# Six of a layer's 391 gathered tiles fetched row by row from the sync queue

## The reference

```python
xw = x @ W                                            # 3125 x (2*128)
xj = xw[src].reshape(-1, H, D) + edge_emb.reshape(-1, H, D)
xi = xw[dst].reshape(-1, H, D)
alpha = leaky_relu(einsum('ehd,hd->eh', xi, att_i) + einsum('ehd,hd->eh', xj, att_j))
ea = exp(alpha - segment_max(alpha, dst)[dst])
alpha = ea / (segment_sum(ea, dst)[dst] + EPS)
aggr = segment_sum(xj * alpha[..., None], dst)        # random rows by src, sums by dst
h = aggr.mean(axis=1) + b                             # relu between layers; self loops are added
```

## Time and profile before

| | |
|---|---|
| median of the runs | 3281.18 us |
| profiled execution | 3286.07 us, of which the span is 3284.3 us |
| TensorE matmul busy | 2403.9 us (73%), mean granted clock 0.543 |
| VectorE busy | 2048.8 us (62%) |
| ScalarE busy | 669.4 us (20%) |
| GpSimd busy | 2140.9 us (65%), of it 1871.6 us in 1955 gathers |
| DMA | 195.81 MB, mean 60 GB/s |

### The profile page before, as it was taken

How to read it: one execution, slowest core, us unless ns; L and a number is a source line. 1 busy time by engine, 2 the same in 40 slices (tenths; PEclk the granted TensorE clock), 3 DMA queues, 4 the chain that set the end, 5 groups by cost and what they waited for, 6 DMA issues and landing times.

```text
span 3284.3 us, 48911 instructions
## 1 busy us (share of the span) xinstructions
PE 2403.9 (73%) x13595; PEld 1980.3 (60%) x13595; DVE 2048.8 (62%) x6821; ACT 669.4 (20%) x3102; POOL 2140.9 (65%) x2357
## 2 busy tenths in 40 slices
PE   6879954778776678768578777857777685778768
PEld 6769933656665456657356656636656573556657
DVE  8965465566576566566656565665565575566567
ACT  0048831111114111110411111131111122111112
POOL 0047737777765777774677777477777747777772
PEclk9555555555557555555755555575555566555556
DMA  3211112222221222221122222122222212222221
GB/s 102 102 69 58 58 51 58 61 60 62 63 51 42 59 64 59 60 64 44 48 64 59 59 66 58 36 59 61 59 62 65 56 36 58 61 62 59 59 56 52
DMA packets 114125, 195.81 MB, mean 60 GB/s; under 512 B 39897, under 2 KB 77272, under 8 KB 113864
## 3 DMA queue, kind: packets, MB, share of 16 engines
q0 software_dynamic: 62560, 130.25, 18.0%
q1 hardware_dynamic: 51304, 62.42, 5.8%
HBM read 180.86 MB, written 11.67 MB: 59 GB/s over the span
## 4 chain that ended last, share of the span: by engine, by line
POOL 50%; issue 18%; DVE 15%; PE 14%; DMA 2%; ACT 1%; DVEq 1%; POOLq 0%; ACTq 0%
POOL ring L512 49%; PE bank L751 6%; PE bank L753 3%; PE bank L724 2%; DVE prod L1079 2%; DVE ring L854 2%; DMA ring<-table,srci 2%; POOL ring L493 1%; DVE ai_rows L947 1%; PE bank L747 1%; DVE y L1361 1%; DVE y L1367 1%; DVE acc L951 1%; DVE prod L1331 1%; PE bank L652 1%
## 5 line engine op out<-in xcount | busy, mean ns | idle before, releaser
L512 POOL DMA_INDIRECT ring<-table,srci x1955 | 1871.6, 957 | 633.6 <-issue 583.0
L751 PE MATMUL bank<-pw,ring 128*128 128x48 f32 x3910 | 1216.9, 411 | 0.0
L751 PEld LDWEIGHTS bank<-pw,ring 128*128 128x128 f32 x3910 | 1009.1, 316 | 103.8 <-issue 23.9
L747 PE MATMUL bank<-zeros 128*128 128x288 bf16 x490 | 209.6, 428 | 595.6 <-DVE pw L1184 595.6
L753 PE MATMUL bank<-onehot,est 128*36 128x24 f32 x3910 | 619.0, 246 | 0.0
L753 PEld LDWEIGHTS bank<-onehot,est 128*36 128x36 f32 x3910 | 382.6, 150 | 177.6
L1128 DVE TENSOR_TENSOR alpha<-alpha,ring 128x56 f32<-128x56 f32 (+7 forms) x75 | 18.1, 241 | 677.1 <-DMA ring<-table,srci 676.9
L747 PEld LDWEIGHTS bank<-zeros 128*128 128x128 bf16 x490 | 54.3, 111 | 638.5 <-DVE pw L1184 603.6
L588 ACT ACTIVATE dd<-dd 128x66 f32<-128x66 f32 x75 | 19.4, 258 | 2004.9 <-DVE dd L1177 2004.9
L1229 DVE TENSOR_TENSOR acc<-acc,bank 128x288 f32 x490 | 222.8, 455 | 267.6 <-PE bank L753 93.3
L582 ACT COPY ai_win<-ai_rows 128x48 f32 x1955 | 309.0, 228 | 136.8 <-DVEq L1116 80.6
(11 more groups left out here) (217 smaller groups left out, 2697.8 us busy)
## 6 DMA issues: line engine op xcount, KB each, us to landing
ring<-table,srci POOLq DMA_INDIRECT x1955
ai_rows<-lo_dram SPq DMA_DIRECT2D x28, 896.0 KB, 4.4
at<-in_attr SPq DMA_DIRECT2D x65, 224.0 KB, 2.9
table<-ring SPq DMA_DIRECT2D x15, 390.0 KB, 3.7
table<-ring SPq DMA_DIRECT2D x5, 325.0 KB, 3.3
result<-ring SPq DMA_DIRECT2D x24, 64.0 KB
x_mid<-ring SPq DMA_DIRECT2D x3, 384.0 KB, 2.7
table<-ring SPq DMA_DIRECT2D x5, 130.0 KB, 2.4
```

The lines of the kernel that those rows point to most:

```text
L512: nc.gpsimd.indirect_dma_start(out=ring[:, slot(t), :], out_offset=None, in_=table, in_offset=bass.IndirectOffsetOnAxis(ap=srci[:, t:t + 1 ...
L747: nc.tensor.matmul(total, zeros[:, 0:P], zeros[:, :], start=True, stop=False, skip_group_check=True)
L751: nc.tensor.matmul(wide[:, 0:H, at_k], ring[:, slot(t), 0:D], pw[:, g % DEEP, k, :, :], start=False, stop=False, skip_group_check=True)
```

## The change

Six tiles of each layer, the last of chunks 1, 3, 5, 7, 9 and 11 (`ROW_TILES`), leave GpSimd's loop, which gathers the other 385. They go into three ring slots of their own; the ring of the gathered tiles has 57 slots instead of 60, so the buffer is as large as before. The sync queue loads them: for each of the 128 edges one DMA of one table row of 520 bytes into one partition, with the row number in a register. The numbers lie in two partitions of `lanes` (`singles`, one more load at the start of the kernel) and are loaded into registers eight at a time. Half a tile (64 row DMAs, 8 register loads) is issued in each of the first twelve steps of the sync queue's loop, ahead of that step's wait. The attribute loads move one step later in that loop, the node weights from c = 9 to c = 12, and the queue waits for its own table writes before the first row. `chain_scan` adds the row tile's terms with an instruction of its own, after a wait for the 128 row DMAs.

```diff
-RING = 60
+RING = 57
+NROWS = 3
+ROW_CHUNKS = (1, 3, 5, 7, 9, 11)
+ROW_TILES = tuple(TC[c + 1] - 1 for c in ROW_CHUNKS)
+GATHERED = [t for t in range(TC[NC]) if t not in ROW_TILES]
+PLACE = {t: p for p, t in enumerate(GATHERED)}
+ROW_STEP = 8
...
 def slot(t):
-    return (t + SHIFT) % RING
+    if t in ROW_TILES:
+        return RING + ROW_TILES.index(t) % NROWS
+    return (PLACE[t] + SHIFT) % RING
...
+            def single_rows(layer, i, half):
+                t, buf = ROW_TILES[i], i % NROWS
+                if half == 0 and i >= NROWS:
+                    sp.wait_ge(sums, layer * G + GROUP_OF[ROW_TILES[i - NROWS]] + 1)
+                r, per = divmod(i, len(ROW_TILES) // 2)
+                for e in range(half * P // 2, (half + 1) * P // 2, ROW_STEP):
+                    _, node = nc.values_load_multi_w_load_instructions(
+                        singles[r:r + 1, per * P + e:per * P + e + ROW_STEP], engines=(mybir.EngineType.SP,),
+                        min_val=0, max_val=N - 1, skip_runtime_bounds_check_because="indices of nodes")
+                    for k in range(ROW_STEP):
+                        sp.dma_start(ring[e + k:e + k + 1, RING + buf, :], table[bass.ds(node[k], 1), :])\
+                            .then_inc(row_gath[buf], 16)
...
             for layer in range(LAYERS):
                 table_tiles(layer)
+                sp.wait_ge(table_w, 16 * (len(TABLE_CUTS) - 1) * (layer + 1))
                 for c in range(NC):
-                    gc = layer * NC + c
-                    if gc + NAT < LAYERS * NC:
+                    gc = layer * NC + c - 1
+                    if c // 2 < len(ROW_TILES):
+                        single_rows(layer, c // 2, c % 2)
+                    if gc >= 0 and gc + NAT < LAYERS * NC:
                         sp.wait_ge(est_ready, gc + 1)
                         attr_chunk(gc + NAT)
...
-                    if c == 9:
+                    if c == 12:
...
-                for t in range(REAL):
-                    if t == RING - SHIFT:
+                for p, t in enumerate(GATHERED):
+                    if p == RING - SHIFT:
                         pool.wait_ge(aj_read, layer + 1)
...
+                if kg < k:
+                    i = ROW_CHUNKS.index(c)
+                    tiles_before = len(ROW_TILES) // NROWS * layer + i // NROWS
+                    v.wait_ge(row_gath[i % NROWS], 16 * P * (tiles_before + 1))
+                    n = V.tensor_tensor(al[:, :, kg:k], al[:, :, kg:k],
+                                        ring[:, slot(TC[c] + kg):slot(TC[c] + kg) + 1, D:ROW]
+                                        .rearrange("p k h -> p h k"), ALU.add)
                 link(n)
```

More of the change, by code:

```diff
@@ L88, with gathered, program @@
 assert len(GC[NC - 3]) == 7 and len(GC[NC - 2]) == 4 and len(GC[NC - 1]) == 3 and DEEP == 6
+def gathered(c):
+    return CH[c] - (c in ROW_CHUNKS)
 def in_class(c, layer):
-    per = sum(CH[k] for k in range(c % NGATH, NC, NGATH))
-    return layer * per + sum(CH[k] for k in range(c % NGATH, c + 1, NGATH))
-def program(nc, x, src_rows, src_key, src_flat, dst_col, dst_next_col, dst_flat, dst_first,
+    per = sum(gathered(k) for k in range(c % NGATH, NC, NGATH))
+    return layer * per + sum(gathered(k) for k in range(c % NGATH, c + 1, NGATH))
+def program(nc, x, src_rows, src_singles, src_key, src_flat, dst_col, dst_next_col, dst_flat, dst_first,
             attr, W1, b1, W2, b2,
@@ L115, in program @@
         ai_rows = sb("ai_rows", [P, H, NP])
-        ring = sb("ring", [P, RING, ROW])
+        ring = sb("ring", [P, RING + NROWS, ROW])
         onehot = sb("onehot", [P, TILES, WIN])
@@ L170, in program @@
         bases = lanes[2 * QB:2 * QB + 1, 0:TILES].bitcast(I32)
+        singles = lanes[QB:QB + 2, 0:len(ROW_TILES) * P // 2].bitcast(I32)
         offs = lanes[3 * QB:3 * QB + 1, 0:TILES].bitcast(I32)
@@ L234, in program @@
         s_parts = part(rowsf, 3 * NT, BF16).rearrange("p (q h) -> p q h", q=3)
-        assert cut[0] <= RING * ROW
+        assert cut[0] <= (RING + NROWS) * ROW
         cut[0] = NT * ROW
@@ L321, in program @@
         gath = [sem(f"gath{i}") for i in range(NGATH)]
+        row_gath = [sem(f"row_gath{i}") for i in range(NROWS)]
+        singles_in = sem("singles_in")
         table_w = sem("table_w")
@@ L383, in _ @@
             sp.dma_start(dstn_i, dst_next_col).then_inc(dst_in, 16)
+            sp.dma_start(singles, src_singles).then_inc(singles_in, 16)
             for dst, s in PRE_LOADS:
@@ L441, in table_tiles @@
                     sp.dma_start(table_pj[:, a:b, :], xt[:, a:b, :]).then_inc(table_w, 16)
+            def single_rows(layer, i, half):
[10 more added lines that the diff above has]
+                            .then_inc(row_gath[buf], 16)
+            sp.wait_ge(singles_in, 16)
             for layer in range(LAYERS):
                 table_tiles(layer)
+                sp.wait_ge(table_w, 16 * (len(TABLE_CUTS) - 1) * (layer + 1))
                 for c in range(NC):
-                    gc = layer * NC + c
-                    if gc + NAT < LAYERS * NC:
+                    gc = layer * NC + c - 1
+                    if c // 2 < len(ROW_TILES):
+                        single_rows(layer, c // 2, c % 2)
+                    if gc >= 0 and gc + NAT < LAYERS * NC:
                         sp.wait_ge(est_ready, gc + 1)
@@ L503, in _ @@
                 pool.wait_ge(table_w, 16 * (len(TABLE_CUTS) - 1) * (layer + 1))
-                for t in range(REAL):
-                    if t == RING - SHIFT:
+                for p, t in enumerate(GATHERED):
+                    if p == RING - SHIFT:
                         pool.wait_ge(aj_read, layer + 1)
[L507 to L510, removed]
+                    if RING - SHIFT <= p < RING - SHIFT + NT:
+                        pool.wait_ge(tr_ps, NT * layer + p - (RING - SHIFT) + 1)
+                    if p >= RING and (p == RING or GROUP_OF[GATHERED[p - RING]] != GROUP_OF[GATHERED[p - RING - 1]]):
+                        pool.wait_ge(sums, layer * G + GROUP_OF[GATHERED[p - RING]] + 1)
                     c = GROUPS[GROUP_OF[t]][0]
@@ L1125, in chain_scan @@
                 al = alpha[:, c % 2, :, 0:k]
-                a = slot(TC[c])
-                split = min(k, RING - a)
+                a, kg = slot(TC[c]), gathered(c)
+                split = min(kg, RING - a)
                 n = V.tensor_tensor(al[:, :, 0:split], al[:, :, 0:split],
                                     ring[:, a:a + split, D:ROW].rearrange("p k h -> p h k"), ALU.add)
-                if split < k:
-                    n = V.tensor_tensor(al[:, :, split:k], al[:, :, split:k],
-                                        ring[:, 0:k - split, D:ROW].rearrange("p k h -> p h k"), ALU.add)
+                if split < kg:
+                    n = V.tensor_tensor(al[:, :, split:kg], al[:, :, split:kg],
+                                        ring[:, 0:kg - split, D:ROW].rearrange("p k h -> p h k"), ALU.add)
+                if kg < k:
[5 more added lines that the diff above has]
+                                        .rearrange("p k h -> p h k"), ALU.add)
                 link(n)
@@ L1377, in _ @@
                     dot(layer + 1, NT - 1, 1, xt[:, NT - 1, D + 1:D + 2])
-_INS = ['x', 'src_rows', 'src_key', 'src_flat', 'dst_col', 'dst_next_col', 'dst_flat', 'dst_first',
+_INS = ['x', 'src_rows', 'src_singles', 'src_key', 'src_flat', 'dst_col', 'dst_next_col', 'dst_flat', 'dst_first',
         'attr', 'W1', 'b1', 'W2', 'b2',
@@ L1415 @@
         x=padded(x, NP, 0),
-        src_rows=src0,
+        src_rows=src0, src_singles=padded(src, slots, 0).reshape(TILES, P)[list(ROW_TILES)].reshape(2, -1),
         src_key=columns(padded(src, slots, 4095)), src_flat=padded(src, slots, 4095).reshape(P, TILES),
```

## The result

The changed kernel takes 3247.43 us (median of four, 3242.21 to 3248.40), against 3281.34 for the kernel before beside it: the ratio is 0.9894, 95% interval 0.9878 to 0.9910, so 1.1% faster. The profiled execution took 3242.21 us, the fastest of the four, with a span of 3240.4.

The account below looks back on a forecast made before the run. GpSimd's gathers up to the end of chunk 12 bound each layer; six fewer save 7.56 us, 37.8 us over five layers, all else costing nothing. Median from 3281.18 to 3243.4 us, range 3237 to 3284, 8 in 10.

Parts of the forecast that it names:

- The bound and the six gathers: GpSimd's gathers up to the end of chunk 12 set a layer's length; six fewer save 7.56 us a layer.
- The ring: GpSimd's gather buffer, 57 slots instead of 60: a slot is needed again 42 gathers later, so it costs nothing.
- VectorE's additions: Thirty extra instructions for row tiles on VectorE, 5.4 us in all, hidden in its idling before the next scan: nothing.
- the disturbance of the gathers: Row DMAs lengthen GpSimd's gathers: 10 ns each gives back 18 us (3261 us), 21 ns the whole gain; chance 0.12.
- The second rival: Row DMAs lengthen GpSimd's gathers through packets on the DMA engines, 10 ns each giving 3261 us; chance 0.12.
- the worst case named with it: All row DMAs run on one DMA engine, the lowest-numbered, making it a fifth busier.
- The price of a row: Sync queue time per row: issue 0.35, arithmetic 0.06, register load 0.04, sum 0.45 us, between 0.41 and 0.69.
- the register load: Loading row numbers on the sync queue, spread over eight rows: 0.04 us a row, between 0.04 and 0.10.
- The cliff: Sync queue: free up to 35.5 us a half (0.548 us a row); beyond, each 0.01 us a row costs 38 us.
- With gaps between halves: Sign of being right: sync queue row DMAs under 0.5 us from one to the next, with pauses between half tiles.
- a queue without gaps: Sign of being wrong: sync queue never pausing over the layer and VectorE waiting for row DMAs from chunk 5 or 7.
- The rule of the Trainium skill: Sync queue: 512 cycles an issue, estimated 0.43 us, puts a row at about 0.57 us, so the change would lose.

Follow-up runs that it names:

- late_six: The kernel before the change with the last six tiles of chunk 13 not gathered, 385 gathers a layer; 3285.71 us, ratio 0.9999 to the kernel before.
- ring57: The kernel before the change with a ring of 57 slots instead of 60, all 391 tiles gathered by GpSimd; 3286.81 us, ratio 1.0003 to the kernel before.
- plain_tile: The changed kernel with each row tile filled by one plain DMA of 128 neighbouring rows instead of 128 row DMAs; 3251.56 us, ratio 0.9898 to the kernel before.
- changed_again: The changed kernel unaltered, measured once more; 3248.31 us, ratio 0.9896 to the kernel before.
- act_rows: The changed kernel with three more row tiles a layer, fetched from ScalarE's queue, and a ring of 55; 3228.59 us, ratio 0.9835 to the kernel before.
- loads12: The changed kernel with twelve register loads for half a tile instead of eight; 3353.10 us, ratio 1.0216 to the kernel before.
- loads10: The changed kernel with ten register loads for half a tile instead of eight; 3244.31 us, ratio 0.9883 to the kernel before.
- eleven: The changed kernel with five more row tiles a layer on ScalarE's queue, numbers loaded by sixteen, ring of 54; 3237.82 us, ratio 0.9868 to the kernel before.

## Why the prediction was right, and where it was not

- **The bound and the six gathers.** Right, in mechanism and size. Forecast 7.56 us a layer; the scan of chunk 12 came 7.1 us earlier in the second layer, the layer took 554.5 us instead of 561.6. Over all five layers the last gather of chunk 12 came 7.8 us earlier in the mean, so nothing of the 7.56 is missing there. `late_six` shows that the place of the gathers counts, and nine and ten row tiles go on by the same 1.26 us a tile. Overall 37.8 us were forecast; the ratio 0.9894 is 34.8 us, its interval 29.5 to 40. Whether 3 us are really missing can't be told from this, as the tails of the layers vary by as much (last section).
- **The ring, VectorE's additions, the disturbance of the gathers.** Right, at nothing each: `ring57` for the first, `plain_tile` against `changed_again` for the row DMAs. The additions weren't tried alone; one took 0.15 us, and they lie in waiting time. The second rival is out for 3840 row DMAs. Its two packets a row were the right number, and its price was not paid: the median gather took 944 ns, as it did in `plain_tile`. Whether all rows ran over one DMA engine, the worst case named with it, no run shows.
- **The price of a row.** Right in outcome, wrong in size: 0.45 us forecast, 0.53 measured. The issue with its arithmetic was well met (0.35 + 0.06 forecast; a half less its loads and the attribute load is about (33.94 - 8 x 0.86 - 0.4) / 64 = 0.42). The term that failed is the register load: I took ScalarE's 0.305 us for four numbers also for eight, 0.04 us a row, over TensorE's 0.77. It takes 0.78 us here, 0.86 with what follows it, 0.11 us a row, a little over the upper bound of 0.10. What I had put down to the engine is mostly the count: on ScalarE itself, in `act_rows`, a load of eight takes 0.83 us at the median and never under 0.72. A row of a load of four says little on one of eight. The loads of eight on ScalarE (ns min/median/max):

```profile
L401 ACTq TENSOR_LOAD <-lanes x240: 722/825/1191, 525.2 to 3124.3; - x120
```

- **The cliff.** Right as a mechanism, and nearer than I said. I saw 0.10 us a row of room and was left with 0.02, 1.6 us in 35.5 a half. `loads12` went over it and lost about what the formula gives for its half; `loads10`, at 35.7, stood on its edge and lost at most a few us. The forecast had 6.3 us of room in a half; that the 1.6 left were enough was in part luck, as a register load 0.2 us longer, eight times, would have used them up.
- **"With gaps between halves".** Wrong. The queue has none in the first twelve chunks. I had named a queue without gaps, together with VectorE waiting for row DMAs, as a sign that the forecast fails; the first alone isn't one. What decides is whether VectorE waits for row DMAs, and it doesn't.
- **The rule of the Trainium skill** ("DMA: Bandwidth & Descriptors", section on why a DMA increments its semaphore by 16): 512 cycles, an estimate of 0.43 us for an issue, would have made the change lose. The row DMAs took 0.225 us at the median, less than either one-row load of the earlier trace rows, and 0.42 from one to the next with its arithmetic; the measurement decides against the page for a copy of one row.

## What to carry over

Where a stream of gathers on one engine bounds a loop, find the last gather that something waits for: taking work out of the stream pays up to that one, at the full pitch, and not behind it. A queue that is otherwise idle can take a share row by row if its issue time for a step, register loads included, stays under the step; price it by the deadline of the consumer, not by the next event on the issuing engine, and keep the last piece well ahead of it, since only there is a late tile without cover.

## What the runs showed of the hardware that was not expected

- A one-row DMA whose source row is in a register costs the sync queue 0.225 us of issue and about 0.42 us from one to the next; a static load of 0.5 KB had 0.29.
- A register load on the sync queue takes 0.78 us for eight numbers and 1.23 for sixteen, against 0.305 for four on ScalarE. ScalarE needs 0.83 for eight (`act_rows`) and 1.29 for sixteen (`eleven`), so between these two queues the count decides. TensorE's 0.766 for three shows that the engine can matter too.
- The tail of a layer has two rhythms, and one execution can have both. In the changed kernel's second layer it took 89.2 us from TensorE's first group of chunk 12 to the next layer, in the third 86.0. In the slower one VectorE's product (line 1112) takes 0.63 us instead of 0.34 in every fourth, eleven times, which makes the 3.2 us; in the faster one VectorE's never does, and GpSimd's addition takes 0.63 us instead of 0.46 each time. The windows, with length, GpSimd's busy time and instructions, granted clock, DMA share and GB/s:

```profile
1494.51:1583.70 89.19, 35.86 (x66) 0.67 0.14 38
2049.23:2135.20 85.97, 39.50 (x66) 0.66 0.15 39
```

The timelines, two instructions of the slower tail and one of the faster:

```profile
1553.41 0.63 DVE L1112 CUSTOM_DVE_ANT_0 prod<-ring,vrow,v 128x128 f32<-128x128 f32 x1
...
1553.43 0.46 POOL L552 TENSOR_TENSOR S<-S 128x128 f32<-128x128 f32 x1
...
2108.25 0.63 POOL L552 TENSOR_TENSOR S<-S 128x128 f32<-128x128 f32 x1
```

The granted clock is the same in both, so it isn't the clock. The step of 3.2 us may be why executions of one kernel lie 3 to 6 us apart; what picks the rhythm is open.
